# Two stacked cross-attention layers on one core: u for two sequences in one product of 512 columns

## The chip, the cores and the metric

The kernel runs on one core of a Trainium2 chip. The core has TensorE (PE, with its weight loads shown apart as PEld), VectorE (DVE), ScalarE (ACT), GpSimd (POOL) and SyncE (SP), which here only issues DMAs. The metric is the device time of one execution in microseconds (us); lower is better. A comparison is made between medians of several executions.

## The reference, cut to what matters

There are 64 sequences of 256 rows. `x` has 512 features, the context `c` 256. Two cross-attention layers follow each other, the second with a softmax over the other axis and a layer norm at its end.

```python
Q = query @ Wq + bq;  K = key @ Wk + bk;  V = key @ Wv + bv          # layer 0
weights = softmax(Q @ K.T * scale, axis=-1)
x1 = query + (weights @ V) @ Wo + bo
q = x1 @ Wq1 + bq1;  k = c @ Wk1 + bk1;  v = c @ Wv1 + bv1           # layer 1
w = softmax(q @ k.T * scale, axis=1)                                 # over the 256 queries
x2 = w @ v + x1
out = (x2 - mean) * rsqrt(var + EPS) * gamma + beta
```

## The kernel before

The products of weights are folded once at the start: A0 = Wq Wk^T, Bv = Wv Wo, A1 and V1 for layer 1. For each sequence there remain, in this order, u = A0^T x^T (+ c0), S0 = u c^T, the softmax E0 of layer 0, Pc = P c, out = Pc Bv, x1, v = A1^T y^T (y is x1), S1 = c v (seeded with g), the softmax w of layer 1, wc = w c, pred = wc V1, x2, and the layer norm. Every fp32 operand of a matmul is split in a high and a low part (`_hi`, `_lo`, type fp32r), and each product is three matmuls (hi hi, hi lo, lo hi; `product`, L390 is the matmul in it). ACT writes the high part with a copy, and the low part is the difference, made by DVE when it comes from PSUM and by POOL when it comes from SBUF.

u of one sequence is 2 halves of its rows (`l`) x 4 tiles of features x 3, that is 24 matmuls with 256 columns moving, into one bank of PSUM (`u_bank`, 512 columns: a half of 256 for each `l`). ACT reads it with `u_h` (L734), DVE with `u_l` (L1030). S0 of the sequence follows later in the same step.

The engines run their own instruction streams and meet by semaphores. The work is a software pipeline written out by hand: `body(r)` is one step. On PE it computes u of sequence r+3, pred of r-1, Pc of r+2, S1 of r, S0 of r+3, out of r+2, v of r+1, wc of r and s of r (the column sums of w; 2 matmuls). There is one `body` for each of PE, ACT, DVE, POOL and SP, with their own order. Steps 0 to 3 are written out, steps 4 to 55 stand in a hardware loop of 13 turns with 4 steps each, 56 to 59 are written out again, and the last four sequences, T(0) to T(3), have a list of calls of their own. So has the start: sequences 0 to 2 enter it one stage after another between the folding of the weights.

The transposes go through DRAM: `E0_blk` is written by 4 DMAs (`write_E0`) and read back as `PT_raw`, `y_blk` as `yT_raw`, `g_blk` as `gT` (128 rows of the same 256 numbers, with which ACT seeds the bank of S1, `S1_seed_`). All of them, the loads and the stores stand in one queue, SP's, in the order of its `body`; an instruction there that waits holds back those behind it. `load_IN` brings x^T (512 KB), c^T and c (256 KB each) of one sequence in a single DMA into `IN`, which has two buffers; `xT` itself (high and low) has one.

## Time and profile before

| what | us |
|---|---|
| median of 3 runs | 1160.12 |
| lowest, highest | 1159.73, 1163.13 |
| the profiled execution | 1160.45 |
| its span (first to last instruction) | 1158.7 |
| busy: PE, PEld | 1139.7, 1060.5 |
| busy: POOL, DVE, ACT | 964.9, 924.6, 892.5 |
| granted clock of PE, mean | 0.996 |
| DMA: bytes, share of the 16 engines | 248.00 MB, 66% |

The durations of single matmuls overlap (0.28 us for one of 256 columns, while starts are 0.12 us apart), so what counts on PE is the distance between starts. A mark in square brackets behind a row of a timeline is idle time of the engine before the instruction and what released it; a row without a mark followed its predecessor at once. The landing of a DMA is counted from its issue.

### The profile page before, as it was taken

To read this page: it belongs to the slowest core of one execution; us is meant where nothing else is said; L and a number is where in the kernel's file an instruction comes from. 1 tells how busy PE (TensorE), PEld (TensorE's weight loads), DVE (VectorE), ACT (ScalarE), POOL (GpSimd) and SP (SyncE) were. 2 spreads that over 40 slices of the span, in tenths; PEclk is the share of its full clock that TensorE was granted. 3 is DMA by queue.
4 is the path that set the end of the run, shared out by engine and by line. 5 is a ranking of instruction groups with operands and counts; after the bars stand their busy time and mean duration, and the time that the engine had idled before them with its cause. 6 is when DMAs were issued, how large, how long until landed. Compare 5 with 4: busy or idle time off the path is not lost.

```text
span 1158.7 us, 25547 instructions
## 1 busy us (share of the span) xinstructions
PE 1139.7 (98%) x7926; PEld 1060.5 (92%) x7926; DVE 924.6 (80%) x2149; ACT 892.5 (77%) x1860; POOL 964.9 (83%) x767
## 2 busy tenths in 40 slices
PE   9999999999999999999999999999999999999996
PEld 6899999999999999999999999999999999999985
DVE  5768778778878778878878888888887887887877
ACT  3568788888788788778778878878878878878764
POOL 2448888888888888888889889889889888888865
PEclk9999999999999999999999999999999999999998
DMA  8466676676676666666667667667667667667541
GB/s 327 155 194 205 212 246 200 223 243 205 213 237 210 214 237 210 217 232 220 215 225 222 217 219 226 213 217 239 203 215 237 210 214 247 205 204 251 171 138 75
DMA packets 130977, 248.00 MB, mean 214 GB/s; under 512 B 15616, under 2 KB 88320, under 8 KB 122624
## 3 DMA queue, kind: packets, MB, share of 16 engines
q1 hardware_dynamic: 129936, 246.54, 65.7%
q10 hardware_dynamic: 1008, 1.06, 0.3%
q8 instruction: 17, 0.28, 0.1%
q14 instruction: 16, 0.13, 0.0%
HBM read 164.63 MB, written 82.90 MB: 214 GB/s over the span
## 4 chain that ended last, share of the span: by engine, by line
PE 94%; DVE 2%; DMA 1%; ACT 1%; issue 1%; SPq 0%; POOL 0%; DVEq 0%; ACTq 0%
PE bank L390 91%; PE bank L471 1%; PE bank L533 1%; PE bank L559 1%; DMA W_s<-in_W 1%; DMA yT_raw<-y_dram 0%; DVE w_lo L1117 0%; DVE R L1064 0%; DVE R L1238 0%; DVE stats L1159 0%; DMA y_dram<-y_blk 0%; ACT Y L853 0%; ACT bank L810 0%; DVE y_blk L1072 0%; DVE scol L1138 0%
## 5 line engine op out<-in xcount | busy, mean ns | idle before, releaser
L1557 POOL TENSOR_TENSOR Y<-Y,gamma_b 128x512 f32<-128x512 f32 x124 | 157.8, 1294 | 18.8 <-ACT Y L853 18.8
L1488 POOL TENSOR_TENSOR xT_lo<-IN,xT_hi 128x1024 fp32r<-128x1024 f32 (+1 forms) x64 | 153.2, 2394 | 22.4 <-ACT xT_hi L700 22.4
L1560 POOL TENSOR_TENSOR Y<-Y,beta_b 128x512 f32<-128x512 f32 x124 | 158.1, 1298 | 0.0
L1488 POOL TENSOR_TENSOR yT_lo<-yT_raw,yT_hi 128x1024 fp32r<-128x1024 f32 x62 | 149.2, 2406 | 4.8 <-ACT yT_hi L700 4.7
L390 PE MATMUL bank<-xT_hi,A_hi 128*128 128x256 f32 x512 | 145.2, 284 | 1.1 <-DVE A_lo L1253 1.1
L390 PE MATMUL bank<-yT_hi,A_hi 128*128 128x256 f32 x512 | 145.2, 284 | 0.0
L390 PE MATMUL bank<-yT_lo,A_hi 128*128 128x256 f32 x512 | 144.9, 283 | 0.0
L390 PE MATMUL bank<-xT_hi,A_lo 128*128 128x256 f32 x512 | 144.5, 282 | 0.0
L390 PE MATMUL bank<-yT_hi,A_lo 128*128 128x256 f32 x512 | 144.4, 282 | 0.0
L390 PE MATMUL bank<-xT_lo,A_hi 128*128 128x256 f32 x512 | 144.3, 282 | 0.0
L1488 POOL TENSOR_TENSOR cT_lo<-IN,cT_hi 128x512 fp32r<-128x512 f32 x64 | 83.4, 1303 | 66.5 <-ACT cT_hi L700 66.5
L700 ACT ACTIVATE bank<-c_b,Z 128x512 f32<-128x512 f32 x128 | 87.8, 689 | 45.4 <-DVE R L1151 44.6
L1151 DVE TENSOR_TENSOR R<-bank,R 128x512 f32<-128x512 f32 x126 | 86.5, 687 | 44.4 <-PE bank L390 44.3
L853 ACT ACTIVATE Y<-R,nmr,rstd 128x512 f32<-128x512 f32 x126 | 95.9, 809 | 20.1 <-POOL nmr L1534 20.1
L1488 POOL TENSOR_TENSOR C_lo<-IN,C_hi 128x512 fp32r<-128x512 f32 x64 | 83.0, 1297 | 32.8 <-ACT C_hi L700 32.8
L700 ACT ACTIVATE bank<-bv_b,scol 128x512 f32<-128x512 f32 x126 | 82.2, 683 | 33.1 <-DVE scol L1138 33.0
L390 PE MATMUL bank<-V_hi,wcT_hi 128*128 128x512 f32 x256 | 101.4, 396 | 2.5 <-ACT bank L700 1.5
L390 PE MATMUL bank<-Bv_hi,PcT_hi 128*128 128x512 f32 x256 | 101.5, 397 | 1.0 <-DVE PcT_lo L1023 1.0
L390 PE MATMUL bank<-Bv_hi,PcT_lo 128*128 128x512 f32 x256 | 100.9, 394 | 0.0
L390 PE MATMUL bank<-V_hi,wcT_lo 128*128 128x512 f32 x256 | 100.7, 393 | 0.0
L390 PE MATMUL bank<-V_lo,wcT_hi 128*128 128x512 f32 x256 | 100.5, 393 | 0.0
L390 PE MATMUL bank<-Bv_lo,PcT_hi 128*128 128x512 f32 x256 | 100.5, 392 | 0.0
(146 smaller groups left out, 4289.6 us busy)
## 6 DMA issues: line engine op xcount, KB each, us to landing
IN<-in_packed SPq DMA_DIRECT2D x63, 1024.0 KB, 7.3
R<-in_x SPq DMA_DIRECT2D x64, 512.0 KB, 3.4
out<-Y SPq DMA_DIRECT2D x63, 512.0 KB, 3.0
y_dram<-y_blk SPq DMA_DIRECT2D x248, 128.0 KB, 2.5
yT_raw<-y_dram SPq DMA_DIRECT2D x62, 512.0 KB, 3.6
E_dram<-E_blk SPq DMA_DIRECT2D x256, 64.0 KB, 1.8
PT_raw<-E_dram SPq DMA_DIRECT2D x64, 256.0 KB, 2.7
gT<-g_dram SPq DMA_DIRECT2D x64, 128.0 KB, 6.8
```

Of the source, the lines that this page charges most:

```text
L390: last = nc.tensor.matmul(dst, stat(a, t), mov(b, t), start=(not seeded and t == 0 and n == 0), stop=(t == k - 1 and n == 2), skip_group_c ...
L471: last = nc.tensor.matmul(s_bank[:, 0:S], ones[:, :], part[:, :], start=(t == 0), stop=(t == 1))
L533: last = nc.tensor.matmul(dst[:, k * L:(k + 1) * L], WqT[:, h, d * P:(d + 1) * P], WkT[:, h, :], start=(k == 0 and h == 0), stop=(h == HT ...
L559: last = nc.tensor.matmul(bank[6 + l][:, :], WvT0_s[:, h, l * P:(l + 1) * P], Wo0_s[:, h, :], start=(h == 0), stop=(h == HT - 1))
L700: return nc.scalar.activation(dst, src, ACT.Copy, **kw)
L853: nc.scalar.activation(Y[n.k % 2][:, q, :], R[n.k % 4][:, q, :], ACT.Identity, bias=nmr[:, q:q + 1], scale=rstd[:, q:q + 1]).then_inc(Y_se ...
L1151: nc.vector.tensor_tensor(R[n.k % 4][:, q, :], pred_bank[q][:, :], R[n.k % 4][:, q, :], ALU.add).then_inc(x2_set, 1)
L1488: return nc.gpsimd.tensor_tensor(dst, src, fp(hi), ALU.subtract)
L1557: nc.gpsimd.tensor_tensor(y[:, q, :], y[:, q, :], gamma_b[:, :], ALU.mult).then_inc(Y_mul, 1)
L1560: last = nc.gpsimd.tensor_tensor(y[:, q, :], y[:, q, :], beta_b[:, :], ALU.add)
```

## The change

u is computed for two sequences at once, n and n+1 with n even. `u_half(r)` gives one half of the rows (`l`) in each step: in an even step the first half of sequences r+4 and r+5, in an odd step the second half of r+3 and r+4. It is 12 matmuls with 512 columns moving, and each half fills `u_bank`, so a half has to be read out before the next begins. Sequences 0 to 3 keep the old form. Step 0 gets a half product of u that it did not have, and the last sequences have none.

For it, x^T is held in two buffers of two sequences (`xTs`), `uT` is twice as wide, and `load_IN` is split in `load_xT` (x^T, 512 KB, into `x_raw`, 7 sequences ahead) and `load_c` (c^T and c, 5 ahead). ACT and POOL convert x^T 6 sequences ahead instead of 4. ACT and DVE read out one half with one instruction of 512 columns; in odd steps near the old place, in even steps late in the step (`u_h_first_half`, `u_l_first_half`). Buffers move in SBUF: some late ones take the room that the weights had at the start. In SP's `body` the read of g goes behind the writes of E0. At the start and in the last four sequences the calls of all engines stand in a new order.

```diff
@@ -92,40 +100,42 @@
         bcol = sb("bcol", [P, 3, HT])
...
+            WqT0_s, WkT0_s = W0_s[:, :, 0:D], W0_s[:, :, D:D + L]
             WqT1_s = sb("WqT1_s", [P, HT, D], where=early)
             WvT0_s = sb("WvT0_s", [P, HT, L], where=early)
             Wo0_s = sb("Wo0_s", [P, HT, D], where=early)
-        Y = [sb(f"Y{n}", [P, ST, D]) for n in range(2)]
+            WkT1_s = sb("WkT1_s", [P, HT, L], where=early)
+            Wv1_s = sb("Wv1_s", [P, LT, D], where=early)
+        w_1 = sb("w_1", [P, S])
+        w_sum = sb("w_sum", [P, S])
+        w_sums = split("w_sums", [P, S])
         w = split("w", [P, ST, S])
         wcT = split("wcT", [P, LT, S])
+        Y = [sb(f"Y{n}", [P, ST, D]) for n in range(2)]
         junk = [sb(f"junk{n}", [P, D]) for n in range(ST)]
-
-        IN = [sb(f"IN{n}", [P, XW + 2 * CW]) for n in range(2)]
-        xT = split("xT", [P, DT, S])
+        PcT = split("PcT", [P, LT, S])
+        yT_raw = sb("yT_raw", [P, NB * ST, DT, 32])
+        R_late = [sb(f"R{n}", [P, ST, D]) for n in (2, 3)]
+
+        x_raw = [sb(f"x_raw{n}", [P, XW]) for n in range(2)]
+        IN = [sb(f"IN{n}", [P, 2 * CW]) for n in range(2)]
+        xTs = [split(f"xT{n}", [P, DT, 2 * S]) for n in range(2)]
         cTs = [split(f"cT{n}", [P, LT, S]) for n in range(4)]
         Cs = [split(f"C{n}", [P, ST, L]) for n in range(4)]
-        R = [sb(f"R{n}", [P, ST, D]) for n in range(4)]
-        uT = split("uT", [P, LT, S])
+        R = [sb(f"R{n}", [P, ST, D]) for n in range(2)] + R_late
+        uT = split("uT", [P, LT, 2 * S])
         vT = split("vT", [P, LT, S])
-        PcT = split("PcT", [P, LT, S])
...
 
+        def u_pair(r):
+
+            return (r.plus(3), 1) if r.odd() else (r.plus(4), 0)
+
+        def own(t, n):
+
+            return t[:, :, n.k % 2 * S:(n.k % 2 + 1) * S]
+
+        def xT_of(n):
+
+            return xTs[n.k // 2 % 2]
+
+        def x_tiles(n):
+            return x_raw[n.k % 2][:, :].rearrange("p (t s) -> p t s", t=DT)
...
@@ -234,21 +260,20 @@
             def weights(dst, src, landed, rows=slice(0, None)):
                 sp.dma_start(dst[:, rows, :], src[:, rows, :]).then_inc(landed, 16)
 
-            def load_IN(n):
+            def load_xT(n):
                 if not n.there():
                     return
                 if n.base is None and n.k == 2:
                     sp.wait_ge(x0_lo, 1)
                 first(sp, xT_lo, n.count(back=2))
+                sp.dma_start(x_raw[n.k % 2][:, :], packed[n.index()][:, 0:XW]).then_inc(xr_in[n.k % 2], 16)
+
+            def load_c(n):
+                if not n.there():
+                    return
                 first(sp, cT_lo, n.count(back=2))
                 first(sp, C_lo, n.count(back=2))
-                sp.dma_start(IN[n.k % 2][:, :], packed[n.index()]).then_inc(in_in[n.k % 2], 16)
-
-            def load_x0():
-                sp.dma_start(IN[0][:, 0:XW], packed[0][:, 0:XW]).then_inc(x0_in, 16)
-
-            def load_c0():
-                sp.dma_start(IN[0][:, XW:XW + 2 * CW], packed[0][:, XW:XW + 2 * CW]).then_inc(in_in[0], 16)
+                sp.dma_start(IN[n.k % 2][:, :], packed[n.index()][:, XW:XW + 2 * CW]).then_inc(in_in[n.k % 2], 16)
 
             def load_x(n):
...
                     sp.dma_start(o_v[T(3).index()][:, q * D:(q + 1) * D], Y[1][:, q, :]).then_inc(y_out[1], 16)
 
             weights(W0_s, W0, w0_in[0], slice(0, 1))
-            load_x0()
             weights(W0_s, W0, w0_in[1], slice(1, 2))
+            load_xT(Seq(0))
             weights(W0_s, W0, w0_in[2], slice(2, 3))
             weights(W0_s, W0, w0_in[3], slice(3, 4))
...
 
             def body(r):
+                load_xT(r.plus(7))
+                load_x(r.plus(2))
                 write_g(r.plus(1))
-                load_x(r.plus(2))
-                load_IN(r.plus(5))
+                load_c(r.plus(5))
+                write_E0(r.plus(3))
                 read_g(r.plus(1))
-                write_E0(r.plus(3))
                 read_E0(r.plus(3))
...
@@ -362,13 +394,13 @@
             load_x(T(2))
             write_g(T(1))
             store(T(-2))
+            write_E0(T(3))
             read_g(T(1))
+            read_E0(T(3))
             load_x(T(3))
-            write_E0(T(3))
             write_y(T(2))
-            read_E0(T(3))
+            read_y(T(2))
             store(T(-1))
-            read_y(T(2))
             write_g(T(2))
...
+            def u_half(r):
+                n, l = u_pair(r)
+                if not n.there():
+                    return
+                if l == 0:
+                    pe.wait_ge(xT_lo, n.plus(1).count())
+                    pe.wait_ge(u_lo, n.count(2, 1, back=1))
+                else:
+                    pe.wait_ge(u_lo, n.count(2, 1))
+                product(u_bank[:, :], lambda a, t: A0[a][:, t, l * P:(l + 1) * P], lambda b, t: xT_of(n)[b][:, t, :], DT
+                        ).then_inc(u_full, 1)
+
             def S0_(n):
                 if not n.there():
                     return
-                pe.wait_ge(u_lo, n.count(2, 1))
+                pe.wait_ge(u_lo, (n if n.one_by_one() or n.odd() else n.plus(1)).count(2, 1))
                 pe.wait_ge(cT_lo, n.count())
                 first(pe, E0_set, n.count(back=1))
                 first(pe, wc_lo, n.count(back=4))
                 for q in range(ST):
-                    last = product(cols(S0_bank, q), lambda a, t: uT[a][:, t, q * P:(q + 1) * P],
...
@@ -633,11 +677,19 @@
             out_(Seq(1), 0)
             out_(Seq(1), 1)
             v_first()
+            Pc_(Seq(2))
+            S0_(Seq(3))
+            S1_(Seq(0))
+            out_(Seq(2), 0)
+            u_half(Seq(0))
+            out_(Seq(2), 1)
+            v_(Seq(1))
+            wc_(Seq(0))
+            s_(Seq(0))
             pe.wait_ge(V1_lo, 1)
 
-            def body(r, u=True):
-                if u:
-                    u_(r.plus(3))
+            def body(r):
+                u_half(r)
                 pred_(r.plus(-1), 0)
...
@@ -658,34 +709,33 @@
             for r in range(LOOP_FROM + 4 * LOOP_TRIPS, NSEQ - 4):
                 body(Seq(r))
 
-            u_(T(3))
+            S0_(T(3))
+            Pc_(T(2))
             pred_(T(-1), 0)
             pred_(T(-1), 1)
-            Pc_(T(2))
-            S0_(T(3))
             S1_(T(0))
+            v_(T(1))
             out_(T(2), 0)
             out_(T(2), 1)
-            v_(T(1))
             wc_(T(0))
             s_(T(0))
             S1_(T(1))
+            Pc_(T(3))
             pred_(T(0), 0)
             pred_(T(0), 1)
-            Pc_(T(3))
-            wc_(T(1))
             out_(T(3), 0)
             out_(T(3), 1)
+            yT_last(0)
...
@@ -707,23 +757,23 @@
             def xT_h(n):
                 if not n.there():
                     return
-                act.wait_ge(in_in[n.k % 2], n.landed(2))
-                first(act, u_full, n.count(back=1))
-                copy(flat(xT[0]), IN[n.k % 2][:, 0:XW]).then_inc(xT_hi, 1)
+                act.wait_ge(xr_in[n.k % 2], n.landed(2))
+                first(act, u_full, n.count(back=3 + n.k % 2))
...
+            def u_half_h(r):
+                n, l = u_pair(r)
+                if not n.there():
+                    return
+                act.wait_ge(u_full, n.plus(l).count())
+                act.wait_ge(S0_full, n.count(back=1))
+                nc.scalar.activation(uT[0][:, l, :], u_bank[:, :], ACT.Identity, bias=c0[:, l:l + 1]).then_inc(u_hi, 2)
+
...
@@ -903,60 +969,64 @@
                 S1_seed_(Seq(0))
 
             xT_h_first()
+            C_h(Seq(0))
             A0_h(0)
             A0_h(1)
             cT_h(Seq(0))
...
             def body(r, prefix=True):
                 if prefix:
                     wc_h(r.plus(-1))
                     pred_seed_(r.plus(-1))
                     PT_h(r.plus(2))
-                    u_h(r.plus(3))
-                xT_h(r.plus(4))
+                xT_h(r.plus(6))
                 if prefix:
                     C_h(r.plus(3))
+                u_h_second_half(r)
+                if prefix:
                     out_seed_(r.plus(2))
                 Pc_h(r.plus(2))
                 yT_h(r.plus(1))
                 exps1(r)
                 exps0(r.plus(3))
                 cT_h(r.plus(4))
+                w_1_(r)
                 w_h(r)
-                w_1_(r)
+                u_h_first_half(r)
                 w_sums_h(r)
                 normalise(r.plus(-1))
...
+            def u_half_l(r):
+                n, l = u_pair(r)
+                if not n.there():
+                    return
+                dve.wait_ge(u_hi, n.plus(l).count(2, 1))
+                nc.vector.scalar_tensor_tensor(uT[1][:, l, :], u_bank[:, :], c0[:, l:l + 1], fp(uT[0][:, l, :]),
+                                               ALU.add, ALU.subtract).then_inc(u_lo, 2)
...
-            def body(r, u=True):
+            def body(r):
                 wc_l(r.plus(-1))
                 dot(r.plus(1), 0)
                 dot(r.plus(1), 1)
                 x2(r.plus(-1), 0)
                 g_blocks(r.plus(1))
-                if u:
-                    u_l(r.plus(3))
+                u_l_second_half(r)
                 x2(r.plus(-1), 1)
                 moments(r.plus(-1))
                 Pc_l(r.plus(2))
@@ -1393,12 +1479,12 @@
                 w_sum_(r)
                 w_l(r)
                 x1(r.plus(2), 1)
+                u_l_first_half(r)
                 y_blocks(r.plus(2))
                 s_columns(r)
                 v_l(r.plus(1))
 
-            body(Seq(0), u=False)
-            for r in range(1, LOOP_FROM):
+            for r in range(0, LOOP_FROM):
                 body(Seq(r))
...
@@ -1491,19 +1576,19 @@
                 if not n.there():
                     return
                 pool.wait_ge(xT_hi, n.count())
-                minus(flat(xT[1]), IN[n.k % 2][:, 0:XW], flat(xT[0])).then_inc(xT_lo, 1)
+                minus(own(xT_of(n)[1], n), x_tiles(n), own(xT_of(n)[0], n)).then_inc(xT_lo, 1)
 
             def cT_l(n):
                 if not n.there():
...
                 scales(r.plus(-1))
@@ -1611,11 +1701,11 @@
             finish(T(-2))
             PT_l(T(2))
             C_l(T(3))
+            yT_l(T(1))
             scales(T(-1))
-            yT_l(T(1))
-            finish(T(-1))
             w_sums_l(T(0))
             PT_l(T(3))
+            finish(T(-1))
             yT_l(T(2))
             w_sums_l(T(1))
```

DVE, the end of one even step (step 2, written out), before; `w_sum` and `w_lo` belong to w of this sequence, `R` to x1, `scol` to s:

```order
L1128 SCALAR_TENSOR_TENSOR w_sum<-bank,rz,w 128x256
L1117 SCALAR_TENSOR_TENSOR w_lo<-bank,rz,w_hi 128x256 x2
L1064 SCALAR_TENSOR_TENSOR R<-bank,rz,R 128x512
L1072 STREAM_TRANSPOSE y_blk<-R 128x8x4x32
L1138 STREAM_TRANSPOSE scol<-bank 32x64 x4
L1023 TENSOR_TENSOR vT_lo<-bank,vT_hi 128x512
L1023 TENSOR_TENSOR wcT_lo<-bank,wcT_hi 128x512
```

and after:

```order
L1213 SCALAR_TENSOR_TENSOR w_sum<-bank,rz,w 128x256
L1202 SCALAR_TENSOR_TENSOR w_lo<-bank,rz,w_hi 128x256 x2
L1149 SCALAR_TENSOR_TENSOR R<-bank,rz,R 128x512
L1107 SCALAR_TENSOR_TENSOR uT_lo<-bank,c,uT_hi 128x512
L1157 STREAM_TRANSPOSE y_blk<-R 128x8x4x32
L1223 STREAM_TRANSPOSE scol<-bank 32x64 x4
L1092 TENSOR_TENSOR vT_lo<-bank,vT_hi 128x512
L1092 TENSOR_TENSOR wcT_lo<-bank,wcT_hi 128x512
```

The low part of the first half of u has come between the second x1 and the transpose to `y_blk`.

SP, one step (step 2, written out), before:

```order
L295 DMA g_dram<-g_blk 4x2x32
L257 DMA R<-in_x 128x1024
L245 DMA IN<-in_packed 128x2048
L301 DMA gT<-g_dram 128x256
L265 DMA E_dram<-E_blk 32x4x128 x4
L273 DMA PT_raw<-E_dram 128x512
L280 DMA y_dram<-y_blk 32x4x256 x4
L308 DMA out<-Y 128x1024
L288 DMA yT_raw<-y_dram 128x1024
```

and after:

```order
L269 DMA x_raw<-in_packed 128x1024
L282 DMA R<-in_x 128x1024
L320 DMA g_dram<-g_blk 4x2x32
L276 DMA IN<-in_packed 128x1024
L290 DMA E_dram<-E_blk 32x4x128 x4
L326 DMA gT<-g_dram 128x256
L298 DMA PT_raw<-E_dram 128x512
L305 DMA y_dram<-y_blk 32x4x256 x4
L333 DMA out<-Y 128x1024
L313 DMA yT_raw<-y_dram 128x1024
```

The load of x^T has an issue of its own at the head, and the read of g has moved from ahead of the four writes of E0 to behind them.

ACT, the start, before (the first conversions, then the high parts of A0, c^T and u of sequence 0):

```order
L700 ACTIVATE xT_hi<-IN 128x1024
L700 ACTIVATE A_hi<-bank 128x512 x2
L700 ACTIVATE cT_hi<-IN 128x512
L734 ACTIVATE uT_hi<-bank,c 128x256 x2
L700 ACTIVATE C_hi<-IN 128x512
```

and after:

```order
L750 ACTIVATE xT_hi<-x_raw 128x4x256
L750 ACTIVATE C_hi<-IN 128x512
L750 ACTIVATE A_hi<-bank 128x512 x2
L750 ACTIVATE cT_hi<-IN 128x512
L784 ACTIVATE uT_hi<-bank,c 128x256 x2
```

C of sequence 0 has moved ahead of both high parts of A0.

## Rows read from the trace of the kernel before

**Rows 1.** The page: busy time of each engine, share of the span, instructions.
```profile
PE 1139.7 (98%) x7926; PEld 1060.5 (92%) x7926; DVE 924.6 (80%) x2149; ACT 892.5 (77%) x1860; POOL 964.9 (83%) x767
```

**Rows 2.** Chain that ended last, in order of time: start us, us, what.
```profile
507.12 17.02 PE bank L390 x120
524.37 17.02 PE bank L390 x120
```

**Rows 3.** Timeline of PE: start us, us, engine line op out<-in [idle before].
```profile
506.96 0.28 PE L390 MATMUL bank<-xT_hi,A_hi 128*128 128x256 f32 x1
...
509.82 0.39 PE L390 MATMUL bank<-V_hi,wcT_hi 128*128 128x512 f32 x1
...
512.60 0.28 PE L390 MATMUL bank<-PT_hi,C_hi 128*128 128x256 f32 x1
```

**Rows 4.** Timeline of DVE in the step that starts at 506.96.
```profile
508.82 0.68 DVE L1023 TENSOR_TENSOR wcT_lo<-bank,wcT_hi 128x512 fp32r<-128x512 f32 x1
...
519.58 0.73 DVE L1064 SCALAR_TENSOR_TENSOR R<-bank,rz,R 128x512 f32<-128x512 f32 x1
520.22 0.24 DVE L1169 BATCH_NORM_AGGREGATE mv<-stats 128x2 f32<-128x6 f32 x2
...
521.94 0.73 DVE L1064 SCALAR_TENSOR_TENSOR R<-bank,rz,R 128x512 f32<-128x512 f32 x1
522.71 1.25 DVE L1072 STREAM_TRANSPOSE y_blk<-R 128x1024 f32<-128x1024 f32 x1
524.41 1.02 DVE L1138 STREAM_TRANSPOSE scol<-bank 32x64 f32<-32x64 f32 x4 [0.45 <-PE bank L471]
```

**Rows 5.** Timeline of the weight loads (PEld) ahead of pred.
```profile
509.69 0.19 PEld L390 LDWEIGHTS bank<-V_hi,wcT_hi 128*128 128x128 f32 x1
```

**Rows 6.** Timeline of ACT in the same step.
```profile
507.18 0.58 ACT L700 ACTIVATE wcT_hi<-bank 128x512 fp32r<-128x512 f32 x1
508.29 1.31 ACT L700 ACTIVATE bank<-bv_b,scol 128x512 f32<-128x512 f32 x2 [0.53 <-DVE scol L1138]
...
521.27 0.42 ACT L700 ACTIVATE w_sums_hi<-w_sum 128x256 fp32r<-128x256 f32 x1 [0.79 <-DVE w_sum L1128]
...
523.84 0.58 ACT L700 ACTIVATE bank<-gT 128x512 f32<-128x512 f32 x1
```

**Rows 7.** Timeline of the SyncE queue in the same step.
```profile
514.39 0.37 SPq L301 DMA_DIRECT2D gT<-g_dram  x1
519.64 1.77 SPq L265 DMA_DIRECT2D E_dram<-E_blk  x4
```

**Rows 8.** Tile gT: its read's time to landing, 500 to 620, then 1110 to 1120.
```profile
DMA to landing us min/median/max: 5.6/6.5/7.7
...
DMA to landing us min/median/max: 2.9/2.9/2.9
```

**Rows 9.** Start: tile IN, issue at 3.11 and its landing; ACT; PE.
```profile
DMA to landing us min/median/max: 9.7/9.7/9.7
...
12.39 0.60 ACT L700 ACTIVATE A_hi<-bank 128x512 fp32r<-128x512 f32 x1 [4.86 <-PE bank L533]
...
14.63 0.38 PE L390 MATMUL bank<-xT_hi,A_hi 128*128 128x256 f32 x1 [1.07 <-DVE A_lo L1253]
```

**Rows 10.** The last four sequences: timelines of PE and POOL.
```profile
1093.57 0.28 PE L390 MATMUL bank<-xT_hi,A_hi 128*128 128x256 f32 x1
...
1109.04 0.28 PE L390 MATMUL bank<-yT_hi,A_lo 128*128 128x256 f32 x1
1109.96 0.38 PE L390 MATMUL bank<-w_hi,C_hi 128*128 128x256 f32 x1 [0.64 <-DVE w_lo L1117]
...
1097.18 1.28 POOL L1488 TENSOR_TENSOR PT_lo<-PT_raw,PT_hi 128x512 fp32r<-128x512 f32 x1
...
1103.48 2.40 POOL L1488 TENSOR_TENSOR yT_lo<-yT_raw,yT_hi 128x1024 fp32r<-128x1024 f32 x1 [0.57 <-ACT yT_hi L700]
```

**Rows 11.** Stretch 59.4 to 62.8: us, busy and instructions by engine, PEclk, DMA share.
```profile
59.40:62.80 3.40, 3.40 (x19) 3.40 (x18) 0.20 (x1) 1.82 (x3) 1.28 (x1) 0.51 0.64 182
```

198 lines of the change are left out of this document (110 added, 88 removed).

## Prediction

> **What bounds the kernel now.** The page's busy times come first [rows 1]: TensorE (PE) is busy 98% of the span, the next engine, GpSimd (POOL), 83%. Busy PE time is not yet proof, since a matmul's end is modelled, so the chain that ended last is read next. In order of time it is one piece of PE work after another, one for each step of the loop (120 matmuls, and 2 for s), and two neighbours start 17.25 us apart [rows 2]. One step is 122 matmuls, and the PE timeline shows them without a gap. So the middle of the kernel, steps 1 to 59, takes what the matmuls' pace takes, and all other engines only have to be in time. The start (to 75 us) and the last four sequences (from 1093.57 us) are bound by chains between engines and have to be read apart.
>
> **What a product with 512 columns costs.** The distance between starts is the price here, not the 0.28 or 0.39 us of one row. The 24 matmuls of u (256 columns) run from 506.96 to 509.82, 2.86 us; the 12 matmuls of pred (512 columns) from 509.82 to 512.60, 2.78 us [rows 3]. These are 119 and 232 ns each: twice the columns cost nearly twice the time, and what is saved is only the small part that each instruction costs by itself. One half of u of two sequences is 12 matmuls of 512 columns, so I price it as pred: 2.78 for 2.86, a gain of 0.08 us in a step. There are 59 such steps (1 to 59): **-4.7 us**. The Trainium skill ("TensorE: Matmul & The Clock Gate", Back-to-back issue gap) gives N/2.4 + 2.5 ns for one matmul; by that, 24 of 256 columns against 12 of 512 save 0.03 us in a step and 1.8 us in all. The trace's own starts carry a larger part for each instruction, and they decide.
>
> **What the middle must still be in time for.** The gain stands only if nobody new is late. Counted from a step's start (506.96):
>
> (a) VectorE (DVE) in even steps. The low part of the first half of u, one instruction of 512 columns, now stands between the second x1 and the transpose to y_blk. The same kind of instruction (R<-bank,rz,R) has its follower 0.64 us later (519.58, 520.22) [rows 4]. Before, y_blk starts 0.77 after x1, of which the last bit is its wait for x1; with u between, it starts 2 x 0.64 after x1, some 0.5 later, at 523.2, and ends at about 524.4. The next instruction, s_columns, starts at 524.41 because it waits for PE's s. So the addition fits in the gap, with nothing to spare. Behind s_columns come vT_lo and wcT_lo (done at 509.50), and pred's first weight load, which needs wcT_lo, starts at 509.69 [rows 5]. The shorter step takes 0.08 from these 0.19 us. About 0.1 us of cover is left in the odd steps. If it goes, the price is the lateness and a restart: the matmul that waited 0.64 us in the tail starts 0.92 after the one before it, where 0.12 is usual, so a wait costs its length and 0.16 more [rows 10].
>
> (b) DVE and ScalarE (ACT) in odd steps. The second half is read out early, as all of u was, one pair of instructions fewer in sum (0.84 us for two of 256, about 0.6 for one of 512), but behind x^T and C on ACT. S0 needs it 8.4 us into the step; it is ready by 6.6. On ACT the first half falls in the 0.79 us in which ACT waited for w_sum (521.27), and it takes 0.58 (the copy of 512 columns out of PSUM) to 0.84 [rows 6]. Free, or 0.05 late for an instruction on which PE does not wait.
>
> (c) The SyncE queue (SP). The read of g stood before the writes of E0, issued at 514.39; now it stands behind them, and they begin when E0_blk is ready at 519.64 and take 1.77 [rows 7]. So it is issued at 521.4, 7 us later. Its time to land was 5.6 to 7.7 us behind the 1 MB load, and 2.9 with nothing before it [rows 8]. In its new place little is queued before it: it lands at 524.3 to 524.9. ACT wants it at 523.84 (bank<-gT), and behind that instruction queue wcT_hi, the seeds of pred and PT. So ACT stalls 0.5 to 1 us. wcT_hi is done at 507.76 and read only at 508.82 by DVE, and pred's first seed (half of the 1.31 us pair from 508.29) is ready at 508.95, where PE takes it at 509.7; this cover is some 0.8 us. I take 2.9 to 3.3, the row of an almost empty queue, and the stall then stays off PE.
>
> (d) GpSimd gets x^T two sequences earlier and in another place of its row of work; the amount is the same, and at 83% busy it has 1.9 us or more of a step to spare. The loads are split in two issues, the bytes stay.
>
> **The start.** ACT now converts C of sequence 0 before the high part of A0. C comes with a load issued at 3.11 us that lands 9.7 later, at 12.8; A0's first half was converted at 12.39 [rows 9]. Now C occupies ACT to 13.45, both halves of A0 follow, and the second ends at 14.5 where it ended at 13.86. The first u waited for just this (14.63, 1.07 us of PE idle). Less the reordered c0 on DVE: **+0.75 us**, and what follows on PE has no idle time to absorb it.
>
> **Step 0 and the last sequences.** Half a product of u is new in step 0: **+2.8**. At the other end u of the last sequence (2.86) is gone: **-2.9**, if the rest keeps its times. It does not. S0 now comes first and takes 1.43; then comes Pc of T(2), which needs PT_lo, done at 1098.46, 4.9 us after the tail's start at 1093.57, since GpSimd finishes two outputs before it [rows 10]. PE idles 3.5 us. Then v of T(1) stands before out, and its yT_lo is done at 1105.88, 12.3 us in. Counted through, out ends 18.0 us in, where all but wc was done at 15.6 before: the tail is 2.4 us behind with 2.9 us less work. Later the new order puts work before waits of the old one (the 0.64 at 1109.96, and seven more marked on PE of 0.2 to 1.0), and wins back about 2.5 to 3. I take **+2.9** for all this, tail unchanged in sum, with bounds of 0 (all of u's time is kept) and +5.2 (nothing is won back). An idle stretch can also cost clock: after PE waited 2.1 us at 56.2, the granted clock was 0.51 from 59.4 to 62.8 [rows 11], 1.7 us of work lost; most of that would lie in the wait for yT_lo.
>
> **Sum**, against the profiled execution (1160.45; its span of 1158.7 and 1.75 around it, 0.3 above the median of 1160.12): -4.7 + 0.75 + 2.8 - 2.9 + 2.9 = -1.15 us. Against the median that is 1159.0.
>
> **The rivals.**
> Gain at the ends kept: the last sequences are not held by PT_lo and yT_lo as I count, or the waits I left in place at the start and in the tail go. For it: eight waits in the tail are there to be filled. Against: GpSimd's finish stands before PT_l in the new order too. Time: 1159.0 - 2.9 = 1156.1, at best 1154.
> DVE late in odd steps, by (a): wcT_lo reaches pred's weight load after the load is due. It decides from 0.1 us of extra delay in s_columns. 30 odd steps x 0.2 to 0.3 us (0.16 and a lateness of up to 0.14) is 6 to 9 us: 1165 to 1168, slower than before. For it: the transpose is pushed by 0.5 us into an instruction that had no slack. Against: s_columns waits for PE anyway.
> g late, by (c): it decides from a landing of 3.7 us. Each further 0.1 us costs 0.1 in every step; 0.3 us is 18 us, 1177. Against it: the stretch before 521.4 has only small writes in flight.
> Weight loads as the bound: with 12 loads fewer in a step and 512 columns hidden behind a load, 12 matmuls would take 12 x 0.119 = 1.43, and 59 steps would save 84 us: 1075. The page has the loads (PEld) busy for 92% of the span, which could be read so. Against it: pred's 12 matmuls also have 12 loads and take 2.78. The Trainium skill ("Perfetto Trace Analysis", Identifying the Most-Contended Engine) names the busy share of weight loads as the measure of how near TensorE is to its limit; by that rule halving u's loads would be worth much more than the starts allow.
>
> **How the numbers follow.** Forecast, the gain of the middle eaten by the ends: 0.50, 1156.8 to 1162. Ends kept: 0.24. DVE late: 0.16. g late: 0.08. Loads as bound: 0.02. A measurement tells about 0.3% (3.5 us) from no change, so faster means below 1156.6. All of "ends kept" but a little, and the lowest edge of the forecast, count as faster: 0.27; the last rival is in it. Slower, above 1163.6: the two late cases, 0.24. Same: 0.49. The range leaves out g late, the loads, and some of the edges: 1154.5 to 1167.
>
> **What would show it.** The period of the chain: 17.17 says the pace, 17.25 or more says a new wait; a period that alternates names the odd steps. Twelve matmuls of u at 232 ns. ACT's bank<-gT waiting on a DMA for 0.5 to 1 us in each step, with PE unmoved. First u at 15.4 instead of 14.63. In the tail, PE idle for 3.5 us before Pc. I am wrong if PE waits in the middle for wcT_lo or a seed, or if the tail (from the S0 that opens it) is shorter than 62 us or longer than 67.5; it was 65.1.

## The result, and the profile of the changed kernel

| kernel | median us | lowest to highest | against before, 95% interval |
|---|---|---|---|
| before | 1160.2 | 1159.7 to 1163.1 | |
| changed | 1184.5 | 1183.8 to 1185.5 | 1.021 (1.0197 to 1.0223) |

The change makes the kernel 24 us slower. Forecast were 1159 us, and at most 1167. The profiled execution took 1183.75 us (span 1182.0, before 1158.7). Cut at the first s and at the s of step 59, as the prediction cut it, the two spans are:

| stretch | before | changed | difference | forecast |
|---|---|---|---|---|
| start to the s of step 0 | 74.9 | 81.0 | +6.1 | +3.55 |
| steps 1 to 59 | 1018.5 | 1031.8 | +13.3 | -4.7 |
| s of step 59 to the end | 65.3 | 69.2 | +3.9 | 0 |

All three parts of the forecast are off, the middle most. The first row of the page answers [rows 1]: TensorE (PE) executes 720 matmuls fewer and has a longer busy time, and the weight loads (PEld) fall from 92% to 87% of the span.

```profile
PE 1152.3 (97%) x7206; PEld 1025.4 (87%) x7206; DVE 923.8 (78%) x2089; ACT 887.8 (75%) x1800; POOL 967.3 (82%) x767
```

The chain that ended last answers [rows 2]. There it was PE alone. Here it leaves PE in nine places, and goes through five other places before it comes back. One of them (start us, us, what):

```profile
240.89 10.16 PE bank L422 x60
251.08 0.70 DVE nmax L1122
252.86 0.72 DVE E_blk L1130
255.49 3.90 DMA gT<-g_dram
259.95 0.59 ACT wcT_hi L750
260.57 0.70 DVE wcT_lo L1092
261.31 14.48 PE bank L422 x96
```

After S0 (the end of the first row) comes the maximum on VectorE (DVE), the blocks of E0, the read of g, wcT_hi on ScalarE (ACT), wcT_lo on DVE, and pred on PE. In the other steps the chain still reads as PE alone, because a matmul that starts 0.1 us late gets no mark. From 200 to 1080 us PE has only three marks (waits: us in total, times, longest), so the loss has to be counted from the starts:

```profile
PE bank L422 <- DVE wcT_lo L1092: 1.0, 3, 0.6
```

The queue shows why a read of g depends on E0. Timeline of SyncE in one step of the middle, where [rows 7] had the read 5.2 us ahead of the writes:

```profile
532.91 1.78 SPq L290 DMA_DIRECT2D E_dram<-E_blk  x4
534.81 0.38 SPq L326 DMA_DIRECT2D gT<-g_dram  x1
536.02 0.34 SPq L298 DMA_DIRECT2D PT_raw<-E_dram  x1
```

The landing of the read answers [rows 8] (tile gT, 500 to 620), and ACT waits for it, with wcT_hi and the seeds of pred (bank<-bv_b,scol) behind it, which answers [rows 6]:

```profile
DMA to landing us min/median/max: 3.4/3.6/3.7
```

```profile
521.02 0.60 ACT L750 ACTIVATE bank<-gT 128x512 f32<-128x512 f32 x1 [1.20 <-DMA gT<-g_dram]
521.56 0.58 ACT L750 ACTIVATE wcT_hi<-bank 128x512 fp32r<-128x512 f32 x1
522.04 1.30 ACT L750 ACTIVATE bank<-bv_b,scol 128x512 f32<-128x512 f32 x2
```

The pair of seeds ends at 523.34, the first of them at about 522.7. u ends before the seed can be used, and pred starts late:

```profile
522.63 0.40 PE L422 MATMUL bank<-xT_hi,A_lo 128*128 128x512 f32 x1
523.00 0.49 PE L422 MATMUL bank<-V_hi,wcT_hi 128*128 128x512 f32 x1
```

These two starts are 0.37 us apart, where 0.23 is usual.

**The ring.** A ring is a chain of waits that comes back to where it began: the read of g waits for E0, E0 for S0, S0 for the pred ahead of it on PE, and that pred for the read of g of the step before. Counted in the timelines of steps 10 to 57, the read of g is issued 2.48 us ahead of s (2.43 to 2.57, since it hangs on S0, which is PE's own work). ACT's copy of gT starts 3.68 us later (3.39 to 4.25), and pred 1.96 after that. So pred starts 3.15 us behind s. PE's own work up to there is s (0.23) and u (2.79), 3.02. That is 0.13 late. Inside pred PE loses another 0.10 (2.88 instead of 2.78), which I put down to the second seed and wcT_lo. Together 0.23 us in a step of 17.45 us. Without it the step would be 17.22. The wait doesn't run out, because a late pred makes S0, E0 and the next read of g late too.

The single steps show the same. Where the time from the issue to the copy of gT is 3.39 us, the step takes 17.19; at 3.66 it takes 17.46, at 3.92 17.69. Fitted to these 48 steps, a step takes 17.22 us and all by which that time exceeds 3.45, one for one. (pred itself starts late from about 3.6 on.)

### The profile page after: what moved, and what is told of

Its sections match the earlier page's. It is cut to its first block, busy times and chain, and to the rows that moved or that the text cites. A ratio compares the mean times of both kernels' runs of the same rounds, so it can differ in the third digit from the quotient of the medians.

```text
span 1182.0 us, 24220 instructions
## 1 busy us (share of the span) xinstructions
PE 1152.3 (97%) x7206; PEld 1025.4 (87%) x7206; DVE 923.8 (78%) x2089; ACT 887.8 (75%) x1800; POOL 967.3 (82%) x767
## 4 chain that ended last, share of the span: by engine, by line
PE 85%; DMA 4%; DVE 4%; issue 2%; ACT 2%; SPq 1%; POOL 1%; POOLq 0%; ACTq 0%; DVEq 0%
PE bank L422 83%; DMA gT<-g_dram 3%; SPq L290 1%; PE bank L515 1%; DMA IN<-in_packed 1%; PE bank L603 1%; DVE nmax L1122 1%; DVE wcT_lo L1092 1%; PE bank L577 1%; ACT wcT_hi L750 0%; DVE E_blk L1130 0%; ACT E L809 0%; DMA x_raw<-in_packed 0%; DVE scol L1223 0%; DVE y_blk L1157 0%
## 5 line engine op out<-in xcount | busy, mean ns | idle before, releaser
L1573 POOL TENSOR_TENSOR xT_lo<-x_raw,xT_hi 128x1024 fp32r<-128x1024 f32 (+1 forms) x64 | 153.2, 2394 | 23.6 <-ACT xT_hi L750 23.6
L422 PE MATMUL bank<-V_hi,wcT_hi 128*128 128x512 f32 x256 | 106.9, 418 | 5.6 <-DVE wcT_lo L1092 4.4
L422 PE MATMUL bank<-xT_hi,A_hi 128*128 128x512 f32 (+1 forms) x272 | 105.4, 388 | 1.5 <-DVE A_lo L1338 1.5
L1573 POOL TENSOR_TENSOR PT_lo<-PT_raw,PT_hi 128x512 fp32r<-128x512 f32 x64 | 82.9, 1296 | 28.5 <-ACT PT_hi L750 27.3
L422 PE MATMUL bank<-xT_hi,A_lo 128*128 128x512 f32 (+1 forms) x272 | 105.1, 386 | 0.0
L422 PE MATMUL bank<-xT_lo,A_hi 128*128 128x512 f32 (+1 forms) x272 | 104.2, 383 | 0.0
L422 PEld LDWEIGHTS bank<-yT_hi,A_hi 128*128 128x128 f32 x512 | 97.5, 190 | 3.3 <-DVE yT_lo L1092 0.8
```

Source lines behind the costliest of these rows:

```text
L422: last = nc.tensor.matmul(dst, stat(a, t), mov(b, t), start=(not seeded and t == 0 and n == 0), stop=(t == k - 1 and n == 2), skip_group_c ...
L1573: return nc.gpsimd.tensor_tensor(dst, src, fp(hi), ALU.subtract)
```

## Experiments

Theory L (loop) says that the ring sets the steps. Its rivals are the late read-out of u from PSUM (R) and the loads in two parts that crowd the queue (C). The parts of the start and the end are tested after it. The columns of the table are the parts of the span as above. They come from one profiled execution each, and in some of these the granted clock fell in the start or the end. So they are to be compared to a microsecond or two there, while the 59 steps have no such fall, but for e3. e1 to e4, e5 to e8 and f1 to f4 were measured at three times, each with the kernel before. So between these groups the ratios to the kernel before are the fairer comparison, and are given where it matters.

| run | median us | start | 59 steps | end |
|---|---|---|---|---|
| before | 1160.2 | 74.9 | 1018.5 | 65.3 |
| changed | 1184.5 | 81.0 | 1031.8 | 69.2 |
| e1, g ahead of E0 | 1167.7 | 79.1 | 1016.4 | 70.8 |
| e2, before, g behind E0 | 1166.2 | 75.8 | 1023.2 | 65.5 |
| e3, g behind the read of E0 | 1271.0 | 80.4 | 1118.0 | 70.8 |
| e4, e1 with 256 columns | 1169.4 | 80.9 | 1018.6 | 68.9 |
| e5, e1 and first loads and copies | 1166.4 | 78.9 | 1016.5 | 68.8 |
| e6, e1 and old end | 1164.3 | 81.3 | 1016.0 | 64.7 |
| e7, e1 and step 0 | 1167.5 | 79.8 | 1016.1 | 68.9 |
| e8, e1 and e5 to e7 | 1163.0 | 79.4 | 1016.8 | 66.3 |
| f1, e8 and old start | 1162.7 | 76.5 | 1016.9 | 66.3 |
| f2, e8 and a filler | 1162.1 | 77.5 | 1016.6 | 64.9 |
| f3, e8 and a split product | 1161.5 | 78.3 | 1016.6 | 64.8 |
| f4, f1 and f3 | 1161.1 | 76.9 | 1017.1 | 64.8 |

**e1: the ring opened.** The changed kernel with one line moved.

```diff
                 load_c(r.plus(5))
+                read_g(r.plus(1))
                 write_E0(r.plus(3))
-                read_g(r.plus(1))
                 read_E0(r.plus(3))
```

> The kernel after, with one edit in SyncE's step: the read of g stands ahead of the four writes of E0 again, as in the kernel before. Theory L (loop): in the kernel after the read of g is issued behind the writes of E0, these wait for E0_blk, E0_blk for S0, S0 for Pc and S1, these for pred, pred for the seeds that ACT writes behind the seed of gT, and that for the read of g of the step before; this ring of waits takes 17.4 us, more than PE's own work. With the read ahead of the writes the ring is open: a step should take 17.17 to 17.20 us (59 steps in 1013 to 1015 instead of 1031.8), and the time should be 1166 to 1168 us; the start (80.9 to the first s) and the end (69.2) stay as they are. Rival R (read-out): the late read-out of u on ACT and DVE sets the steps; then they stay at 17.44 and the time at 1184. Rival C (the loads in two parts crowd the queue or the DMA engines): the same, 1184, with the landing of gT 3.6 us or more.

Measured: 1167.7 us, 1.0067 of before (1.0048 to 1.0085). The 59 steps take 15.4 us less than in the changed kernel. A step takes 17.227 us on average; 17.17 to 17.20 was expected. The copy of gT no longer has a mark, though the landing is the same, because the read is issued 4.3 us earlier against s (6.8 instead of 2.5 us ahead):

```profile
526.81 0.58 ACT L750 ACTIVATE bank<-gT 128x512 f32<-128x512 f32 x1
527.33 0.58 ACT L750 ACTIVATE wcT_hi<-bank 128x512 fp32r<-128x512 f32 x1
528.56 1.30 ACT L750 ACTIVATE bank<-bv_b,scol 128x512 f32<-128x512 f32 x2 [0.65 <-DVE scol L1223]
```

```profile
DMA to landing us min/median/max: 3.1/3.5/3.9
```

The late read-out of u (R) and the loads in two parts (C) are still in this kernel, and the steps are short. So neither costs the 13 us by itself. The seeds now wait for DVE's scol (0.65), not for a DMA.

**e2: the ring in the kernel before.** The same line moved the other way, and nothing else.

```diff
-                read_g(r.plus(1))
                 write_E0(r.plus(3))
+                read_g(r.plus(1))
                 read_E0(r.plus(3))
```

> The kernel before, with one edit in SyncE's step: the read of g goes behind the four writes of E0; u stays in its old form of one sequence with 256 columns. Theory L: the ring of waits is closed here too; with a landing of 2.9 to 3.6 us a step should take 17.3 to 17.5 us instead of 17.25, that is 3 to 15 us more, 1163 to 1175 us, and ACT should wait for gT in each step. Rivals R and C (the cost comes from the new u or the split loads): 1160, steps of 17.25.

Measured: 1166.2 us, 1.0054 of before (1.0037 to 1.007), steps of 17.345 us in the middle where all were 17.25. One cause, put in alone, gives an effect of the same kind. ACT waits for gT in each of 29 steps (waits of the stretch 500 to 1000: us in total, times, longest):

```profile
ACT bank L700 <- DMA gT<-g_dram: 30.4, 29, 1.2
```

But it is smaller: the 59 steps get 4.7 us longer, where the same line makes 15.4 in the changed kernel (against e1). The steps say why. The copy of gT starts 3.52 us behind the issue here (changed: 3.68). Up to 3.47 a step takes 17.25 as before (17.33 once), and at 3.6 to 3.7 some 17.4. So the threshold is nearly the same in both kernels, and what exceeds it is 0.1 us on average here and 0.23 there. What in the changed kernel makes the landing 0.16 us later was not tested; the loads in two parts (C) may have this share in it.

**e3: one place later.** It gives the ring a known dose.

```diff
                 write_E0(r.plus(3))
-                read_g(r.plus(1))
                 read_E0(r.plus(3))
+                read_g(r.plus(1))
```

> The kernel after, with the read of g one place later: behind the read of E0 too. It is issued 1.6 us later than in the kernel after (the read of E0 waits for the writes' landing: 536.02 against 534.81, and its issue takes 0.34). Theory L: every microsecond in the ring is a microsecond in each step: 17.44 + 1.6 = 19.0 us, or up to 19.5 if the landing behind a larger read grows by 0.5; in 59 steps 94 to 122 us more, 1280 to 1305 us. Rivals R and C: the read has slack or is not the cause, and the time moves by less than 20 us.

Measured: 1271.0 us in its only execution, a little under the range that was expected. The read is issued 0.81 us ahead of s instead of 2.48, that is 1.67 later, and the seed follows the issue by 3.26 instead of 3.68 us. The difference, 1.25 us, added to 17.45 is 18.70. Steps 10 to 57 take 18.77 (median 18.69). All 59 steps average 18.95, since six of them take 20.9 to 23.1 us: behind PE's wait the granted clock fell there (0.66 from 182 to 192 us). So a part of the 86 us in the table is the clock. The chain that ended last now goes through the read of g 48 times, where it was nine. The landing got shorter, where the expectation had it longer:

```profile
DMA to landing us min/median/max: 2.9/3.2/4.1
```

Each microsecond in the ring is one in the step. With e1, which opens the ring, and e2, which puts it into the kernel before, that settles theory L.

**e4: what 512 columns are worth.** e1 with the same half product in 24 matmuls of 256 columns.

```diff
-                product(u_bank[:, :], ..., lambda b, t: xT_of(n)[b][:, t, :], DT
-                        ).then_inc(u_full, 1)
+                for h in range(2):
+                    last = product(u_bank[:, h * S:(h + 1) * S], ...,
+                                   lambda b, t: xT_of(n)[b][:, t, h * S:(h + 1) * S], DT)
+                last.then_inc(u_full, 1)
```

> As e1_g_ahead, with the half product of u as 24 matmuls of 256 columns (the two sequences one behind the other, same banks and waits) in place of 12 of 512. It measures what 512 columns are worth by themselves. From the starts of the matmuls (0.119 us apart at 256 columns, 0.232 at 512) 24 x 0.119 - 12 x 0.232 = 0.07 us a step, 4 us in all: steps of 17.24 to 17.27 against 17.17 to 17.20, and the time 4 us above e1_g_ahead. If the number of weight loads counted for more than the columns, the difference would be larger: 12 more loads beside matmuls of 0.119 us. If 512 columns bring nothing, the two are equal.

Measured: 1169.4 us, steps of 17.253 us, as in the kernel before, and 1.7 us above e1 in the medians (the lowest of e1 is 1165.9, its highest 1170.4). In steps 10 to 58 u takes 2.861 us with 256 columns and 2.798 with 512, so the product gains 0.063 us, close to the 0.07 of the starts. But v, whose instructions are the same, takes 2.869 us instead of 2.845, out 2.796 instead of 2.784, and pred 2.789 instead of 2.779 (Pc wins 0.009). A net gain of 0.026 us is left in each step, 1.5 us in 59. What makes v longer is not shown. e2, with 256 columns, has v at 2.859, so the number of columns is not needed for it. The weight loads were no bound: halving those of u (PEld 91% in e4, 88% in e1) brings only this.

**e5 and e7: the start.** e5 loads x^T of sequence 0 ahead of the second quarter of W0 again and moves ACT's copy of C behind u; DVE and POOL follow. The diff below shows ACT's part. e7 has, in step 0, Pc ahead of x^T of sequence 6.

```diff
             xT_h_first()
-            C_h(Seq(0))
             A0_h(0)
             A0_h(1)
             cT_h(Seq(0))
             u_h_first()
+            C_h(Seq(0))
```

> As e1_g_ahead, and at the very start the order of the kernel before: x^T of sequence 0 is loaded ahead of the second quarter of W0, ACT copies C of sequence 0 behind the first u instead of ahead of A0, and DVE and POOL follow. Theory S: these two put the first matmul of u at 15.56 us instead of 14.63 and TensorE idle for 1.54 us ahead of it instead of 1.07; with the old order it starts at 14.6, and the first s comes 0.9 us earlier, 78.2 against 79.1 in e1_g_ahead; time 1166.8. In executions where the granted clock fell to 0.7 behind that idle time (the kernel after and e4_two_256: first s at 80.9) the gain would be up to 2.8 us. Rival: what is won at 15 us is lost again in the wait for x_raw at 66.78 us, which hangs on the queue; then the first s stays at 79.1.

> As e1_g_ahead, and in step 0 alone ACT copies Pc of sequence 2 ahead of x^T of sequence 6. In e1_g_ahead ACT waits at 66.78 us for the landing of x_raw, Pc_hi comes behind it (67.75), PcT_lo behind that, and TensorE is idle for 1.76 us ahead of out. Expected: that idle time goes, the first s at 77.3 to 78 us instead of 79.1, the time 1166 to 1166.6. Rival: x^T of 6 or yT is then late in its turn (yT_raw lands at 70.08), and the first s stays at 79.

In the changed kernel C, whose load lands late, holds up A0 on ACT, and the first u starts at 15.56 us behind 1.54 us of idle time, instead of 14.63 behind 1.07, which answers [rows 9]:

```profile
13.07 0.63 ACT L750 ACTIVATE C_hi<-IN 128x512 fp32r<-128x512 f32 x1 [3.98 <-DMA IN<-in_packed]
13.61 1.07 ACT L750 ACTIVATE A_hi<-bank 128x512 fp32r<-128x512 f32 x2
```

```profile
15.56 0.39 PE L422 MATMUL bank<-xT_hi,A_hi 128*128 128x256 f32 x1 [1.54 <-DVE A_lo L1338]
```

Then the granted clock fell. Stretches 14 to 22 us of the changed kernel and of the kernel before (us, then busy us of PE, PEld, DVE, ACT, POOL, then the granted clock as a share of 2.4 GHz, the DMA share and GB/s):

```profile
14.00:18.00 4.00, 2.46 (x17) 2.44 (x17) 1.36 (x3) 1.19 (x3) 2.75 (x4) 0.87 1.02 417
18.00:22.00 4.00, 4.00 (x15) 2.82 (x14) 1.09 (x3) 1.97 (x4) 0.00 (x0) 0.70 1.02 418
```

```profile
14.00:18.00 4.00, 3.37 (x25) 3.15 (x26) 0.57 (x1) 0.52 (x2) 1.72 (x3) 1.00 1.04 430
18.00:22.00 4.00, 4.00 (x17) 2.31 (x16) 3.24 (x4) 3.38 (x6) 2.50 (x2) 1.00 0.99 416
```

A share of 0.70 is a mixture of the two levels, 1.2 and 2.4 GHz. The first u took 4.17 us (15.56 to 19.73) instead of 2.95. Only the idle time tells the order of the copies here, not the start of u: e2, whose start is that of the kernel before, has its first u at 15.53, behind the same 1.07. In e5 the idle time is 1.07 again, the first u starts at 14.79 and the clock is at 1.00. But the first s comes only 0.2 us earlier than in e1, whose clock had not fallen there either. That is the rival of the expectation: ACT waits for x_raw in both, and copies it at 66.58 us (e1: 66.78). The medians differ by 1.3 us, and the executions of both spread over 4.6 us and more, so this test is weak. In e7 the wait of 1.76 us ahead of out is gone, as expected, and x_raw is still waited for, behind Pc now:

```profile
67.03 0.60 ACT L750 ACTIVATE PcT_hi<-bank 128x512 fp32r<-128x512 f32 x1 [0.84 <-PE bank L422]
68.50 1.06 ACT L750 ACTIVATE xT_hi<-x_raw 128x1024 fp32r<-128x1024 f32 x1 [0.87 <-DMA x_raw<-in_packed]
```

Its median is equal to that of e1 within the spread. The first s at 79.8 us says little, since the clock in its stretch 14 to 22 was 0.78, and that of e1 1.00. No gain of e7 can be shown.

**e6: the end.** e1 with the last four sequences in the order of the kernel before on all engines, without u of the last one (which the wide product already contains).

> As e1_g_ahead, and the last four sequences in the order of the kernel before on all five engines, without the calls for u of the last sequence. Theory T: the new order of the end costs time by itself. From the last step's s to the end it took 69.2 us (kernel after) and 70.8 us (e1_g_ahead), and the kernel before took 65.3 with 24 matmuls of u in it, that is 2.9 us more work; with the old order 62.4 to 63.5 us are expected, and a time of 1160 to 1161.5 us. Rival: the end is longer because S0 of the last sequence and its E0 come under the same late values of g and wc, whatever the order; then it stays at 69 us or more, and the time at 1167.

Measured: 1164.3 us, 3.4 below e1 and 2.8 above the upper end of what was expected. The end takes 64.7 us, not 62.4 to 63.5. The order did cost, but the 2.9 us of u that were taken out did not come back. Of the 6.1 us between the ends of e1 and e6 (70.8 and 64.7) a part is the clock: it was 0.50 and 0.66 from 1100 to 1108 in e1, some 3 us of work by my estimate, and did not fall in e6. The next runs show where the 2.9 us went.

**e8: all together.**

> e1_g_ahead, e5_start, e6_end and e7_step0 together: the wide u, with the read of g ahead of the writes of E0 and the start and the end in the old order. If the parts add up: first s at 77 to 77.5 us (before: 74.9, with 12 matmuls of u, 2.8 us, less in it), 59 steps in 1016.4 us (before 1018.5), the end 62.5 us (before 65.3 with 2.9 us of u in it): a span of 1156 to 1156.5 and a time of 1157.7 to 1158.5 us, 0.15% below the kernel before. If the end or the start is long for another reason than its order, 1160 to 1167.

Measured: 1163.0 us (1159.9 to 1164.3 in 11 executions), 1.0016 of before (1.0007 to 1.0025), and above the 1157.7 to 1158.5 that were expected from the sum of the parts. Ahead of the first pred of the end PE now stands idle, for the seed of pred:

```profile
1099.00 0.50 PE L422 MATMUL bank<-V_hi,wcT_hi 128*128 128x512 f32 x1 [2.44 <-ACT bank L750]
```

```profile
1096.20:1100.20 4.00, 1.56 (x9) 1.18 (x8) 3.50 (x11) 3.30 (x6) 4.00 (x5) 1.00 0.88 284
1100.20:1104.20 4.00, 4.00 (x16) 3.36 (x15) 1.82 (x4) 0.81 (x2) 2.29 (x2) 0.57 0.88 272
```

In the kernel before, u of the last sequence ran in this place, and nothing waited. In this execution the clock fell behind the idle time, to 0.57 over 4 us. In e6 the same wait of 2.44 us was followed by 1.00.

**f2: a filler.** e8 with that product put back, its result unused.

```diff
+            fill_()
             pred_(T(-1), 0)
             pred_(T(-1), 1)
             Pc_(T(2))
```

> As e8_all, with 24 matmuls of 256 columns (2.86 us, the size and the place of the product u that the change takes away from the last sequence) between the last step's s and pred; their result is not used. Theory F: the removed product had covered a wait (TensorE idle for 2.44 us there in e6_end and e8_all, for the seed of pred and wcT), so what the steps were given for it is not given back; filled again it costs 0.4 us at most, and the granted clock, which falls to 0.71 for 6 us behind that idle time in e8_all, stays at 1.00. So the end takes 64.7 to 65.5 us (e8_all 66.3, before 65.3) and the time is 1161.5 to 1163.4. Rival: that product was work on the path, and 2.86 us more work gives 2.86 us more: the end 69 us, time 1165.8.

Measured: 1162.1 us with 2.86 us more work, 1.0018 of before (1.0009 to 1.0026), where e8 has 1.0016: no difference. The end takes 64.9 us (65.3 before). e6, with the wait and without a fall of the clock, took 64.7, so this is the fairer comparison: 2.86 us more work for 0.2 us. The wait and the fall of the clock are both gone:

```profile
1094.10:1098.10 4.00, 4.00 (x32) 3.83 (x31) 3.48 (x10) 3.33 (x6) 4.00 (x5) 1.00 0.85 275
1098.10:1102.10 4.00, 4.00 (x27) 3.65 (x26) 2.85 (x6) 1.85 (x4) 2.40 (x2) 1.00 0.85 260
```

So u of the last sequence was no work on the path. It covered a wait of 2.4 us, and taking it away earns nothing.

**f3 and f1.** f3 moves real work there: in step 59 only the part of sequence 62 is computed (12 matmuls of 256 columns), and that of sequence 63 behind the s of step 59.

```diff
             def body(r):
-                u_half(r)
+                if r.base is None and r.k == NSEQ - 5:
+                    u_last(0)
+                else:
+                    u_half(r)
...
+            u_last(1)
             pred_(T(-1), 0)
```

> As e8_all, and the second half product of the last two sequences (12 matmuls of 512 columns in step 59) is split: the part of sequence 62 stays in step 59 (12 of 256), the part of sequence 63 goes behind the last step's s, ahead of pred (12 of 256, 1.43 us). No work is added. Theory F: the idle time of 2.44 us shrinks to 1.0 us while step 59 gets shorter by 1.4 us; step 59 and the end together take 1.4 us less than in e8_all (17.2 + 66.3), up to 3 us less where the clock no longer falls, and the time is 1160 to 1161.6. Rival (work on the path): nothing changes, 1163.

Measured: 1161.5 us, 1.0013 of before (1.0004 to 1.0022), within the noise of e8. The idle time ahead of pred is 1.01 us, as expected. But step 59 did not get 1.4 us shorter. It takes 17.15 us (e8: 17.19), because with half of u gone from it, the same wait opens ahead of its own pred:

```profile
1080.59 0.50 PE L422 MATMUL bank<-V_hi,wcT_hi 128*128 128x512 f32 x1 [1.01 <-ACT bank L764]
1097.74 0.50 PE L422 MATMUL bank<-V_hi,wcT_hi 128*128 128x512 f32 x1 [1.01 <-ACT bank L764]
```

Step 59 and the end together take 81.9 us, as in e6 (17.19 and 64.7). What the profile has less than e8 there, 1.6 us, is the clock, which did not fall. So moving the work gained nothing that shows; u covers such a wait in every step, and taking half of it away uncovers it.

f1 is e8 with the copies and low parts of the start in the old order on ACT, DVE and POOL. x^T of 4 and 5 stand behind cT of 3 and at the end of the start's list.

> As e8_all, with the whole start on ACT, DVE and POOL in the order of the kernel before, and x^T of 4 and 5 (of which the kernel before converts one less there) put at late places. In e8_all PT_raw of sequence 0 is copied at 38.26 us (before: 35.09) and TensorE waits 1.64 us for PT_lo at 40.28; exps0 of sequence 0 and its blocks stand behind C and Bv there. Theory S2: it is this order; with the old one that wait goes, the first s comes at 77.7 to 78.5 us (before 74.9 and 2.8 of the half product more) against 79.4 in e8_all, and the time is 1.5 us lower, 1161.5 against 1163.0. Rival: the order of the loads in the queue sets it (x^T and WqT1 in a new sequence, which this kernel keeps); then the first s stays at 79.4 and the time at 1163.

Measured: the first s at 76.5 us, earlier than expected, and the wait of 1.64 us at 40.28 is gone. But the median is 1162.7, 0.3 below e8 and inside the spread, and the ratio is 1.0021 (1.0012 to 1.003). In f3, which keeps the start of e8, the same wait was 0.77 us. The profiled execution of e8 was its slowest and that of f1 one of its fastest, so the traces exaggerate this part.

**f4: both.**

> f1_old_start and f3_split_last together: the wide u with everything that was found to cost taken back. If both add up: first s at 78, 59 steps in 1015 us, the end at 64.5 us: a time of 1158.5 to 1160, between 0.15% faster than the kernel before and equal to it. If the gains of the start and the end overlap or are lost: 1161 to 1163. Either way the product of 512 columns by itself is worth 1.5 to 2 us of 1160.

Measured: 1161.1 us (1160.3 to 1161.8), ratio 1.0003 (0.9995 to 1.0012). That is no difference from the kernel before. The changed form of u, with everything that was found around it taken back, neither gains nor costs.

## Why the prediction was wrong

**The step that failed is (c), the read of g.** It was said to stay off PE, and priced at nothing. The mechanism stood in the text, as a term and as a rival: issue behind the writes, ACT stalled, wcT_hi and the seeds behind it, 0.1 us a step for each 0.1 us beyond a landing of 3.7. The size was off twice. For the landing I took 2.9 to 3.3 us, "the row of an almost empty queue", from the end of the kernel [rows 8], for a read that stands right behind four writes. It takes 3.6 there (3.4 to 4.2), and ACT's copy follows within 0.1. And the threshold was 3.45, not 3.7. The 3.7 does not even follow from the text's own numbers: issued at 521.4, wanted at 523.84 and with a cover of 0.8, the read may take 3.24. The average stayed 0.23 us beyond the threshold, and that was lost in each of 59 steps. I had placed the landing at its cheap end; with a slope of 6 us for each 0.1 us, 0.08 was too small a chance for it. The text also treated 0.8 us of cover as a reserve, and did not follow the read back to see that its issue hangs on PE by S0. A lateness there is fed back, not absorbed once. Of the middle's miss of 18.0 us (+13.3 instead of -4.7), 15.4 are this read (e1 takes them away); the rest is the pace.

**The pace.** u of 512 columns saves 0.063 us, not 0.08, and 0.037 of it is lost in v, out and pred: -1.5 us in 59 steps (e1 against e4), where -4.7 was forecast. The estimate by the rule of the Trainium skill ("TensorE: Matmul & The Clock Gate", Back-to-back issue gap), 1.8 us in all, is near the net result. That is luck: the rule gives 0.03 us for the product, which gained 0.063, and knows nothing of what the others lost. For the product the starts of the trace were the better price.

**(a), DVE.** Nearly right. In e1 the transposes to scol follow y_blk at once, without the mark of [rows 4]. What is lost ahead of pred is 0.01 us in a step.

```profile
525.56 0.73 DVE L1107 SCALAR_TENSOR_TENSOR uT_lo<-bank,c,uT_hi 128x512 fp32r<-128x512 f32 x1
526.22 1.23 DVE L1157 STREAM_TRANSPOSE y_blk<-R 128x1024 f32<-128x1024 f32 x1
527.42 1.02 DVE L1223 STREAM_TRANSPOSE scol<-bank 32x64 f32<-32x64 f32 x4
```

Even and odd steps differ by 0.015 us in e1, so the rival of a late DVE in odd steps did not come. (b) and (d) held: from 200 to 1080 us of e1 no wait of PE is marked.

**The start**, +6.1 instead of +3.55: 2.8 of the half product and 0.93 of the late first u were forecast in kind (+0.75), though of the 0.93 only 0.47 is longer idle time, and the old start alone came at 14.63 in one execution and at 15.53 in another (e2). Not forecast were 1.2 us of a lower clock behind the longer idle time and 0.94 us of a wait for Pc, which ACT copies behind x^T of sequence 6 and its DMA:

```profile
68.62 1.06 ACT L750 ACTIVATE xT_hi<-x_raw 128x1024 fp32r<-128x1024 f32 x1 [2.29 <-DMA x_raw<-in_packed]
69.59 0.58 ACT L750 ACTIVATE PcT_hi<-bank 128x512 fp32r<-128x512 f32 x1
```

```profile
70.94 0.51 PE L422 MATMUL bank<-Bv_hi,PcT_hi 128*128 128x512 f32 x1 [0.94 <-DVE PcT_lo L1092]
```

I had read the start's order on ACT for its first entries only, and priced no new DMA wait at step 0.

**The end**, +3.9 instead of 0. The term -2.9 for u of the last sequence was wrong in kind: it had covered the wait for wcT and the seed (f2). I had put the idle time of the new order at Pc, 3.5 us. It comes one place earlier, at S0, which waits for wcT_lo and, like all steps, for g. The granted clock falls behind it as well, to 0.68 from 1115 to 1118:

```profile
1115.93 0.42 PE L422 MATMUL bank<-cT_hi,uT_hi 128*128 128x256 f32 x1 [2.78 <-DVE wcT_lo L1092]
```

```profile
1112.00:1115.00 3.00, 1.15 (x10) 0.95 (x8) 2.36 (x6) 1.72 (x5) 3.00 (x3) 1.00 0.84 187
1115.00:1118.00 3.00, 2.06 (x10) 2.10 (x11) 2.15 (x6) 2.33 (x5) 2.15 (x3) 0.68 0.98 295
```

The rivals "gain at the ends kept" and "weight loads as the bound" are refuted. By the rule in the Trainium skill ("Perfetto Trace Analysis", Identifying the Most-Contended Engine) the weight loads' share tells how near TensorE is to its limit. Here it would have misled: from e4 to e1 the share fell from 91% to 88%, and a step gained 0.026 us, where this rival had 1.43.

## What to carry to other kernels

When an issue is moved in a queue, follow it back to what it now waits for and forward until the chain closes. If the bounding engine is in that ring, there is no reserve to spend, only a threshold, and everything beyond it is paid in every turn; price it by the row that has the same neighbours in the queue, not by the cheapest. Work that is taken out just ahead of a wait earns nothing until the wait goes too (e6), and work moved from one such place to another opens the same wait there (f3). And a short idle stretch can be paid a second time, through the lower clock behind it.
